# Second layer's context attention: row maxima passed through DRAM to all partitions, second scores one step later

## Chip, cores and metric

One core of a Trainium2 chip runs the kernel. The metric is the device time of one execution in microseconds.

## What is computed

Two layers of a Perceiver on 8 batches of 128 latent rows of width 512, with a context of 2048 rows a batch. The change lies in the second layer's attention from the latents to the context, 16 heads of 32:

```
q = query @ Wq.T + bq;  k = key @ Wk.T + bk;  v = value @ Wv.T + bv
scores = einsum('bhtd,bhsd->bhts', q, k) / sqrt(32)
attn = softmax(scores, axis=-1)
out = einsum('bhts,bhsd->bhtd', attn, v) @ Wo.T + bo
```

`query` is the normalised state x, `key` and `value` are the context, and the result is added to x.

## The kernel before

`softmax_context` (L1228) cuts the work into 32 units (`NU`): a batch b and a group g of four heads (`HG` = 4, r below). A unit has four chunks c of 512 context rows, so there are 128 steps n = 4u + c. All arithmetic is fp32. Each engine walks a list of tiles that `pe_step` (L1288), `act_step` (L1298) and `dve_step` (L1304) write out by step; semaphores join them.

TensorE's step: "score" (L1484), the scores of the four heads with the queries on the partitions, four matmuls of 512 columns into the four banks `score[r]`; "key" (L1540) of the next unit; in the first step of a unit "spread" (L1557) of the unit before; "score_t" (L1501), the same scores again of the unit before with the keys on the partitions, 16 products into the same four banks; "value" (L1548) of the next unit; "attend" (L1518), five steps behind its scores (`LAG`). "sums" (L1560) come in a unit's second step, "output" (L1575) in the third step of a batch's second unit, "hidden" and "query" in the third unit. A score waits for the shift that read its bank, a second score for the maximum that did.

Why twice: the softmax needs each query's maximum. "max" (L1423) takes minus the maximum of each chunk on VectorE, one number a query, so a partition. The second scores have queries along the free dimension, so the maxima must stand along it, on every partition. "diagonal" (L1427) takes the minimum over the chunks, multiplies it into the identity, and the spread multiplies ones by that diagonal: a bank with each row's number on all partitions, which ScalarE copies into `shift` (L1398). "shift" (L1435) then adds it to the second scores on VectorE, 128x512 a head, into `weights_t` (3 slots), "exp" (L1394) raises them on ScalarE in place, attend uses them, and GpSimd adds them up over the context into `partial` (L1384 to L1388), two units deep. The sums of that, by TensorE, are inverted in "heads" (L1447), which also frees `attended` for the next unit.

Keys, spreads, values, sums and the rest pass through one ring of three banks. Keys have 9 slots, values 12. In 56 of the 128 pairs of unit and chunk the values were made in earlier layers, and SyncE loads them from DRAM (`load_values`, L1334), 256 KB a pair; it also loads the next batch's context, 1 MB a chunk.

Of the kernel before, what the change touches and what calls it, by code (L numbers as in the profile page):

```python
# [16 lines left out]
P = 128  # L17
B = 8
D = 512
# [174 lines left out]
def broadcast(row):  # L194

    return row.partition_broadcast(P)
# [1031 lines left out]
def softmax_context(nc, x_sb, ident, a, ahead, own, later):  # L1228
# [7 lines left out]
    KEYS, VALUES, SLOTS = 9, 12, 3  # L1236
    with ExitStack() as ctx:
# [10 lines left out]
        diagonal = s.sb("diagonal", [P, HG, P])  # L1248
        shift = s.sb("shift", [P, 2, HG, P])
# [21 lines left out]
        diagonal_set = s.sem("diagonal_set")  # L1271
# [3 lines left out]
        value_landed = [s.sem(f"value_landed{n}") for n in range(4)]  # L1275
        chain, chain_pool = s.sem("chain"), s.sem("chain_pool")
        LOADS = 3 + 1
        LAG = NCH + 1
# [9 lines left out]
        def pe_step(n):  # L1288
            u, c = divmod(n, NCH)
            b, g = divmod(u, NG)  # L1290
            out = [("score", u, c)] * (u < NU) + [("key", u + 1, c)] * (u + 1 < NU)
            out += [("sums", u - 2)] * (c == 1 and u >= 2) + [("spread", u - 1)] * (c == 0 and 1 <= u <= NU)
            out += [("score_t", u - 1, c)] * (1 <= u <= NU) + [("value", u + 1, c)] * (u + 1 < NU)
            out += [("attend", (n - LAG) // NCH, (n - LAG) % NCH)] * (0 <= n - LAG < NU * NCH)
            out += [("hidden", b + 1)] * (g == 2 and c == 1 and b + 1 < B) + [("query", b + 1)] * (g == 2 and c == 2 and b + 1 < B)
            return out + [("output", b - 1)] * (g == 1 and c == 2 and b >= 1)

        def act_step(n):  # L1298
            u, c = divmod(n, NCH)
            exps = [("exp", u - 1, c, r) for r in range(HG)] * (1 <= u <= NU)  # L1300
            out = [("key", u + 1, c)] * (u + 1 < NU) + [("spread", u - 1)] * (c == 0 and 1 <= u <= NU)
            return out + exps[:2] + [("value", u + 1, c)] * (u + 1 < NU) + exps[2:]

        def dve_step(n):  # L1304
            u, c = divmod(n, NCH)
            b, g = divmod(u, NG)
            out = [("max", u, c, r) for r in range(HG)] * (u < NU) + [("heads", u - 2)] * (c == 1 and u >= 2)
            out += [("shift", u - 1, c, r) for r in range(HG)] * (1 <= u <= NU)
            out += [("diagonal", u)] * (c == NCH - 1 and u < NU)
            out += [("norm", b + 1)] * (g == 1 and c == 0 and b + 1 < B)  # L1310
            out += [("later", b - 1)] * (g == 1 and c == 3 and b >= 1)
            out += [("hidden", b + 1)] * (g == 2 and c == 1 and b + 1 < B) + [("query", b + 1)] * (g == 2 and c == 2 and b + 1 < B)
            return out + [("output", b - 1)] * (g == 1 and c == 2 and b >= 1)
# [9 lines left out]
                          lambda t: "a" if t[0] in ("key", "value", "spread") else "d")  # L1323

        with nc.Block() as block:

            @block.sync
            def _(sp):
# [5 lines left out]
                def load_values(k):  # L1334
# [5 lines left out]
                    if k >= 4:  # L1340
                        sp.wait_ge(value_landed[k % 4], 16 * (k // 4))
                    if n >= VALUES:
# [3 lines left out]
                                 ahead.dram[j][:, g * D:(g + 1) * D]).then_inc(value_landed[k % 4], 16)  # L1346
# [44 lines left out]
            def _(act):  # L1391
                for t in act_steps:
# [21 lines left out]
            def _(dve):  # L1414
# [5 lines left out]
                for t in dve_steps:  # L1420
# [6 lines left out]
                    elif what == "diagonal":  # L1427

                        dve.wait_ge(maxed, (u + 1) * NCH * HG)
                        link(nc.vector.tensor_reduce(row_min[:], neg_max[:, e], AX.X, ALU.min))  # L1430
                        if u:
                            dve.wait_ge(full_a, ring.count(("spread", u - 1)))
                        nc.vector.tensor_tensor(diagonal[:], ident[:].unsqueeze(1).broadcast_to([P, HG, P]),
                                                row_min[:].unsqueeze(2).broadcast_to([P, HG, P]), ALU.mult).then_inc(diagonal_set, 1)
                    elif what == "shift":  # L1435
# [3 lines left out]
                        if c == 0 and r == 0:  # L1439
                            dve.wait_ge(out_a, ring.count(("spread", u)))  # L1440
                        if n >= SLOTS and r == 0:
# [4 lines left out]
                                                shift[:, e, r, :].unsqueeze(1).broadcast_to([P, DC, P]), ALU.add).then_inc(shifted, 1)  # L1446
# [31 lines left out]
            def _(pe):  # L1478
# [3 lines left out]
                for t in pe_steps:  # L1482
                    what, u = t[0], t[1]
                    if what == "score":  # L1484
# [6 lines left out]
                        for r in range(HG):  # L1491
                            rows = slice(r * HD, (r + 1) * HD)
                            if n > NCH:

                                pe.wait_ge(shifted, (n - NCH - 1) * HG + r + 1)
                            elif n:
                                pe.wait_ge(maxed, (n - 1) * HG + r + 1)
# [3 lines left out]
                    if what == "score_t":  # L1501
# [3 lines left out]
                        for k in range(DC):  # L1505
                            for r in range(HG):
                                rows = slice(r * HD, (r + 1) * HD)
                                if k == 0 and u + 1 < NU:

                                    pe.wait_ge(maxed, (n + NCH) * HG + r + 1)  # L1510
# [7 lines left out]
                    if what == "attend":  # L1518
                        c = t[2]
                        n = u * NCH + c  # L1520
                        if (u, c) in load_no:
                            k = load_no[(u, c)]
                            pe.wait_ge(value_landed[k % 4], 16 * (k // 4 + 1))
# [644 lines left out]
```

## Time and profile before

| | |
|---|---|
| median of 3 runs | 4110.35 us (4109.7 to 4110.72) |
| the profiled execution | 4110.32 us |
| its span | 4108.5 us |
| busy over the span | TensorE 3995.8, VectorE 2177.3, ScalarE 1270.8, GpSimd 1003.8 us |
| first key to last output of this layer | about 2519 to 3819 us |

The span is what the instructions cover; 1.8 us lie around it. The busy shares are means over seven stages with different limits, so the stage itself is looked at: which engine has no idle time in it, and which waits end last. Times in the rows are from the span's start. A row of the order in time that merges several instructions runs from the first one's start to the last one's end.

### The profile page before, as it was taken

Reading aid. Unit: us, or ns where it says so; the run is one execution under the profiler, and the core shown is the slowest. Engines: PE = TensorE matmul, PEld = TensorE weight load, DVE = VectorE, ACT = ScalarE, POOL = GpSimd, SP = SyncE. Lnnn points to the kernel's source line nnn. Section 1 sums busy time; section 2 is a strip of 40 time slices with the busy share of each in tenths; the row PEclk is TensorE's granted clock in tenths of the full one; section 3 lists DMA queues with packets and bytes.
Section 4 is the critical chain, followed back from the end, with each engine's and each line's share of the span. In section 5 each row is a group of like instructions: output and inputs, shape, how many; then the busy total and the mean of one; then the engine's idle time right before and its main releaser. Section 6 shows DMA issues by size and latency. Waiting matters only on the chain. (4 is left out here: it accounts for less than half of the span.)

```text
span 4108.5 us, 73501 instructions
## 1 busy us (share of the span) xinstructions
PE 3995.8 (97%) x30656; PEld 2736.5 (67%) x30656; DVE 2177.3 (53%) x4381; ACT 1270.8 (31%) x3156; POOL 1003.8 (24%) x831
## 2 busy tenths in 40 slices
PE   8999999999999999899899999999999999998897
PEld 4777777777777778677465445666666666666675
DVE  5555555555555555255544324566665665546356
ACT  2222222222323222144233100333333333333344
POOL 2020202020202020022211000454454454445322
PEclk9999999999999999999999999999999999999899
DMA  4111111111111122211311400101101101101000
GB/s 144 62 62 62 62 62 62 62 62 62 62 61 63 58 66 73 88 29 35 108 42 48 163 0 29 55 24 45 58 24 45 58 25 45 50 1 45 11 2 21
DMA packets 127303, 219.86 MB, mean 54 GB/s; under 512 B 9088, under 2 KB 47616, under 8 KB 125184
## 3 DMA queue, kind: packets, MB, share of 16 engines
q1 hardware_dynamic: 118272, 181.60, 13.5%
q0 software_dynamic: 8704, 33.56, 2.5%
q8 instruction: 247, 4.05, 0.4%
q14 instruction: 80, 0.66, 0.1%
HBM read 198.35 MB, written 16.78 MB: 52 GB/s over the span
## 5 line engine op out<-in xcount | busy, mean ns | idle before, releaser
L577 PE MATMUL swishmax_attended<-swishmax_weights_t,swishmax_context 128*128 128x128 f32 x4096 | 520.1, 275 | 3.4 <-DVE swishmax_values_t L505 3.4
L1386 POOL TENSOR_TENSOR context_partial<-context_partial,context_weights_t 128x512 f32<-128x512 f32 x320 | 404.6, 1264 | 470.4 <-ACT context_weights_t L1397 452.7
L577 PEld LDWEIGHTS swishmax_attended<-swishmax_weights_t,swishmax_context 128*128 128x128 f32 x4096 | 487.9, 192 | 3.9 <-issue 3.9
L1546 PE MATMUL context_bank<-ahead_stream,ahead_staged 128*128 128x512 f32 x1024 | 473.3, 605 | 1.3 <-PEq L1072 1.3
L591 PE MATMUL swishmax_bank<-ahead_stream,ahead_w 128*128 128x512 f32 x1024 | 464.0, 596 | 7.2 <-DMA ahead_stream<-in_context_t_dram 7.2
L1445 DVE TENSOR_TENSOR context_weights_t<-context_score,context_shift 128x512 f32<-128x512 f32 x512 | 317.7, 683 | 231.9 <-PE context_score L1513 231.9
L435 ACT ACTIVATE swishmax_xes<-swishmax_score,swishmax_neg_max 128x512 f32<-128x512 f32 x256 | 177.2, 694 | 808.2 <-DVE swishmax_neg_max L470 808.2
L1426 DVE TENSOR_REDUCE context_neg_max<-context_score 128x1 f32<-128x512 f32 x512 | 317.9, 683 | 161.7 <-PE context_score L1498 161.4
L577 PE MATMUL swishmax_attended<-swishmax_weights_t,swishmax_sides 128*128 128x128 f32 x3072 | 384.9, 275 | 0.0
L1546 PEld LDWEIGHTS context_bank<-ahead_stream,ahead_staged 128*128 128x128 f32 x1024 | 184.0, 189 | 279.8 <-issue 272.2
L577 PEld LDWEIGHTS swishmax_attended<-swishmax_weights_t,swishmax_sides 128*128 128x128 f32 x3072 | 363.6, 192 | 0.0
L1397 ACT ACTIVATE context_weights_t<-context_weights_t 128x512 f32<-128x512 f32 x512 | 304.9, 629 | 181.8 <-DVE context_weights_t L1445 181.8
L591 PEld LDWEIGHTS swishmax_bank<-ahead_stream,ahead_w 128*128 128x128 f32 x1024 | 186.0, 192 | 198.8 <-issue 196.5
L409 POOL TENSOR_TENSOR swishmax_values_t<-swishmax_pair 128x256 f32<-128x256 f32 x32 | 23.4, 730 | 1172.3 <-ACT swishmax_pair L452 1172.2
L1405 ACT ACTIVATE context_keys_t<-context_bank,context_bias 128x512 f32<-128x512 f32 x128 | 88.0, 687 | 665.4 <-PE context_bank L1546 600.2
L1555 PE MATMUL context_bank<-ahead_w,ahead_stream 128*128 128x128 f32 x2304 | 290.4, 280 | 0.0
L1555 PEld LDWEIGHTS context_bank<-ahead_w,ahead_stream 128*128 128x128 f32 x2304 | 267.5, 192 | 18.3 <-issue 3.8
L470 DVE TENSOR_REDUCE swishmax_neg_max<-swishmax_score 128x1 f32<-128x512 f32 x256 | 164.7, 685 | 121.4 <-PE swishmax_score L562 121.4
L597 PEld LDWEIGHTS swishmax_bank<-whole_ident,swishmax_xes 128*128 128x128 f32 x1024 | 115.0, 141 | 163.7 <-issue 96.1
L475 DVE TENSOR_TENSOR swishmax_xes<-swishmax_xes,swishmax_score 128x512 f32<-128x512 f32 x256 | 175.5, 687 | 66.3 <-ACT swishmax_xes L435 66.3
L1513 PEld LDWEIGHTS context_score<-context_queries_t,context_keys_t 32*128 32x128 f32 x4096 | 132.6, 188 | 84.1 <-issue 69.9
L1387 POOL TENSOR_TENSOR context_partial<-context_partial,context_weights_t 128x512 f32<-128x512 f32 x128 | 164.3, 1284 | 10.0
(341 smaller groups left out, 5768.9 us busy)
## 6 DMA issues: line engine op xcount, KB each, us to landing
ahead_stream<-in_context_t_dram SPq DMA_DIRECT2D x78, 1024.0 KB, 5.8
swishmax_context<-in_context_dram POOLq DMA_DIRECT2D x32, 1024.0 KB, 5.9
swishmax_down<-_L_xattn_value_down_dram SPq DMA_DIRECT2D x64, 256.0 KB, 4.3
swishmax_up<-in_L_xattn_value_up_dram SPq DMA_DIRECT2D x32, 512.0 KB, 6.2
ahead_values<-ahead_staged SPq DMA_DIRECT2D x14, 1024.0 KB, 8.8
context_values<-ahead_values SPq DMA_DIRECT2D x56, 256.0 KB, 3.3
experts_w<-in_L_ffn_W_dram SPq DMA_DIRECT2D x16, 512.0 KB, 8.1
whole_x<-in_x_dram SPq DMA_DIRECT2D x8, 256.0 KB, 9.2
```

The lines of the kernel that those rows point to most:

```text
L435: nc.scalar.activation(xes[:, n % XES, r, :], score[r][:], ACT.Exp, bias=neg_max[:, e, r, c:c + 1]).then_inc(exped, 1)
L470: nc.vector.tensor_reduce(neg_max[:, e, r, c:c + 1], score[r][:], AX.X, ALU.max, negate=True).then_inc(maxed, 1)
L475: nc.vector.tensor_tensor(xe, xe, score[r][:], ALU.mult).then_inc(weighted, 1)
L577: last = nc.tensor.matmul(product(i)[:, m, :], side(left, c, k, m), weights_t[:, n % 2, right, k, :], start=c == 0 and k == 0 and m == 0 a ...
L591: last = nc.tensor.matmul(bank_t[:], w_key[:, k, g * P:(g + 1) * P], context_t[:, c, k, :], start=k == 0, stop=k == DC - 1)
L1386: link(nc.gpsimd.tensor_tensor(acc, acc, w_t[:, :, k, :], ALU.add))
L1387: nc.gpsimd.tensor_tensor(acc, acc, w_t[:, :, DC - 1, :], ALU.add).then_inc(summed, 1)
L1397: nc.scalar.activation(weights_t[:, n % SLOTS, r], weights_t[:, n % SLOTS, r], ACT.Exp).then_inc(exped, 1)
L1426: nc.vector.tensor_reduce(neg_max[:, e, r, c:c + 1], score[r][:], AX.X, ALU.max, negate=True).then_inc(maxed, 1)
L1445: nc.vector.tensor_tensor(weights_t[:, n % SLOTS, r], score[r][:].rearrange("p (k q) -> p k q", q=P), shift[:, e, r, :].unsqueeze(1).broad ...
L1546: last = nc.tensor.matmul(bank_t[:], w["k"][:, k, g * P:(g + 1) * P], context_t[:, c, k, :], start=k == 0, stop=k == DC - 1)
L1555: last = nc.tensor.matmul(bank_t[:, i * P:(i + 1) * P], context_t[:, c, k, m * P:(m + 1) * P], w["v"][:, k, g * P:(g + 1) * P], start=k == ...
```

## The change

The maxima reach the free dimension through DRAM. VectorE's "minima" step keeps the reduction into `row_min` and makes no diagonal. ScalarE's queue issues two DMAs a unit: `row_min`, 16 bytes from each of 128 partitions, to a 2 KB line in DRAM, at the start of the next unit's first step; and that line to all partitions (256 KB) into `shift`, behind that step's exponentials. The spread on TensorE and its copy on ScalarE are gone, and the ring has one tile a unit fewer. `shift` is laid out by query and then head, where it was by head and then query, so the shift reads it with a stride of four numbers. Second scores, shifts, exponentials and attend come one step later; a tenth slot of keys covers that. Sums and heads go from a unit's second to its third step, output from the third to the fourth, the gathering for the next part from the fourth to the next unit's first. The loads of values alternate between two semaphores, not four.

```diff
-    KEYS, VALUES, SLOTS = 9, 12, 3
+    KEYS, VALUES, SLOTS = 10, 12, 3
...
-        diagonal = s.sb("diagonal", [P, HG, P])
-        shift = s.sb("shift", [P, 2, HG, P])
+        minima_dram = nc.dram_tensor("context_minima", (NU, P, HG), F32, kind="Internal").ap()
+        shift = s.sb("shift", [P, 2, P, HG])
...
-        LAG = NCH + 1
+        LAG = NCH + 2
...
-            out += [("sums", u - 2)] * (c == 1 and u >= 2) + [("spread", u - 1)] * (c == 0 and 1 <= u <= NU)
-            out += [("score_t", u - 1, c)] * (1 <= u <= NU) + [("value", u + 1, c)] * (u + 1 < NU)
+            out += [("sums", u - 2)] * (c == 2 and u >= 2)
+            out += [("score_t", *divmod(n - NCH - 1, NCH))] * (0 <= n - NCH - 1 < NU * NCH) + [("value", u + 1, c)] * (u + 1 < NU)
...
+            minima = [(what, u - 1) for what in ("minima_out", "minima_in")] * (c == 0 and 1 <= u <= NU)
+            out = [("key", u + 1, c)] * (u + 1 < NU)
+            return minima[:1] + out + exps[:2] + [("value", u + 1, c)] * (u + 1 < NU) + exps[2:] + minima[1:]
...
-                    if k >= 4:
-                        sp.wait_ge(value_landed[k % 4], 16 * (k // 4))
+                    if k >= 2:
+                        sp.wait_ge(value_landed[k % 2], 16 * (k // 2))
...
-                    elif what == "spread":
-                        act.wait_ge(full_a, ring.count(t))
-                        nc.scalar.copy(shift[:, u % 2], ring.bank(t)[:].rearrange("p (r q) -> p r q", q=P)).then_inc(out_a, 1)
+                    elif what == "minima_out":
+                        act.wait_ge(minima_set, u + 1)
+                        act.dma_start(minima_dram[u], row_min[:]).then_inc(minima_landed, 16)
+                    elif what == "minima_in":
+                        act.wait_ge(minima_landed, 16 * (u + 1))
+                        act.dma_start(shift[:, u % 2].rearrange("p q r -> p (q r)"),
+                                      broadcast(minima_dram[u].rearrange("q r -> (q r)"))).then_inc(shift_landed, 16)
...
                         if c == 0 and r == 0:
-                            dve.wait_ge(out_a, ring.count(("spread", u)))
+                            dve.wait_ge(shift_landed, 16 * (u + 1))
...
-                                                shift[:, e, r, :].unsqueeze(1).broadcast_to([P, DC, P]), ALU.add).then_inc(shifted, 1)
+                                                shift[:, e, :, r].unsqueeze(1).broadcast_to([P, DC, P]), ALU.add).then_inc(shifted, 1)
...
-                    elif what == "spread":
-                        pe.wait_ge(diagonal_set, u + 1)
-                        last = nc.tensor.matmul(bank_t[:], ones[:], diagonal[:].rearrange("p r q -> p (r q)"), start=True, stop=True)
```

## Rows read from the trace of the kernel before

**Rows 1.** busy us by engine (count) in a stretch, granted clock, DMA share, GB/s.

```profile
2620.00:3740.00 1120.00, 1119.88 (x11774) 697.87 (x11776) 664.93 (x1115) 396.55 (x712) 540.61 (x426) 1.00 0.13 39
```

**Rows 2.** TensorE in order of time: start us, us, engine, line, tiles, shape, count.

```profile
2906.89 1.14 PE L1498 MATMUL context_score<-context_keys_t,context_queries_t 32*128 32x512 f32 x8
...
2915.69 1.14 PE L1498 MATMUL context_score<-context_keys_t,context_queries_t 32*128 32x512 f32 x8
...
2921.25 1.17 PE L1513 MATMUL context_score<-context_queries_t,context_keys_t 32*128 32x128 f32 x32
...
2924.34 1.08 PE L1532 MATMUL context_attended<-context_weights_t,context_values 128*32 128x128 f32 x32
...
2925.35 1.14 PE L1498 MATMUL context_score<-context_keys_t,context_queries_t 32*128 32x512 f32 x8
...
2934.50 0.66 PE L1567 MATMUL context_bank<-whole_ident,context_hidden 128*128 128x128 f32 x4
```

**Rows 3.** VectorE in order of time, the same steps; in brackets the idle time before.

```profile
2922.44 2.48 DVE L1445 TENSOR_TENSOR context_weights_t<-context_score,context_shift 128x512 f32<-128x512 f32 x4 [3.03 <-PE context_score L1513]
...
2932.06 2.48 DVE L1445 TENSOR_TENSOR context_weights_t<-context_score,context_shift 128x512 f32<-128x512 f32 x4
```

**Rows 4.** TensorE by tile: duration in ns min/median/max, first and last start us.

```profile
L1559 PE MATMUL context_bank<-context_diagonal,context_ones x64: 592/592/697, 2577.0 to 3781.8; 128*128 128x512 f32 x64
...
L1498 PE MATMUL context_score<-context_keys_t,context_queries_t x1024: 587/692/1217, 2546.4 to 3773.2; 32*128 32x512 f32 x171
```

**Rows 5.** ScalarE in order of time, the same steps.

```profile
2924.71 1.15 ACT L1397 ACTIVATE context_weights_t<-context_weights_t 128x512 f32<-128x512 f32 x2
```

**Rows 6.** VectorE by line, small instructions elsewhere, strided or not; ns as in 4.

```profile
L1154 DVE TENSOR_TENSOR experts_gap<-experts_best x2: 165/165/165, 2289.4 to 2407.1; 128x4 f32<-128x4 f32 x2
...
L1159 DVE TENSOR_TENSOR experts_prob<-experts_prob,experts_gap_exp x2: 163/164/164, 2294.3 to 2412.9; 128x4 f32<-128x4 f32 x2
...
L1788 DVE TENSOR_SCALAR features_half_norm<-features_bank x16: 183/186/193, 3839.6 to 4029.5; 128x16 f32<-128x16 f32 x16
...
L1144 DVE COPY experts_gate<-experts_bank_d x8: 166/167/168, 2285.3 to 2405.6; 128x8 f32<-128x8 f32 x8
...
L1781 DVE TENSOR_SCALAR features_inverse<-features_bank x8: 276/278/291, 3872.8 to 4062.0; 128x128 f32<-128x128 f32 x8
```

**Rows 7.** DMA issues: target, queue, count, KB, us to landing; last, value loads min/median/max.

```profile
ahead_stream<-in_context_t_dram SPq DMA_DIRECT2D x78, 1024.0 KB, 5.8
context_values<-ahead_values SPq DMA_DIRECT2D x56, 256.0 KB, 3.3
...
context_bias_o<-in_L_xattn_bo_dram SPq DMA_DIRECT2D x1, 256.0 KB, 5.0
context_bias<-in_L_xattn_bq_dram SPq DMA_DIRECT2D x1, 2.0 KB, 1.8
...
DMA to landing us min/median/max: 2.9/3.3/8.2
```

**Rows 8.** the value loads' issuing instruction on SyncE, ns min/median/max.

```profile
L1345 SPq DMA_DIRECT2D context_values<-ahead_values x56: 319/320/573, 2521.5 to 3531.2; - x56
```

**Rows 9.** the layer's end in order of time: TensorE, VectorE, GpSimd.

```profile
3752.58 2.73 PE L1513 MATMUL context_score<-context_queries_t,context_keys_t 32*128 32x128 f32 x32
...
3777.84 2.48 DVE L1445 TENSOR_TENSOR context_weights_t<-context_score,context_shift 128x512 f32<-128x512 f32 x4 [1.76 <-PE context_score L1513]
...
3783.49 2.48 DVE L1445 TENSOR_TENSOR context_weights_t<-context_score,context_shift 128x512 f32<-128x512 f32 x4 [2.36 <-PE context_score L1513]
...
3793.43 2.48 DVE L1445 TENSOR_TENSOR context_weights_t<-context_score,context_shift 128x512 f32<-128x512 f32 x4 [1.59 <-PE context_score L1513]
3796.96 2.48 DVE L1445 TENSOR_TENSOR context_weights_t<-context_score,context_shift 128x512 f32<-128x512 f32 x4 [1.04 <-PE context_score L1513]
...
3803.46 3.94 POOL L1386 TENSOR_TENSOR context_partial<-context_partial,context_weights_t 128x512 f32<-128x512 f32 x3
3807.47 1.26 POOL L1387 TENSOR_TENSOR context_partial<-context_partial,context_weights_t 128x512 f32<-128x512 f32 x1
```

More of the change, by code:

```diff
@@ L1291, in pe_step @@
             out = [("score", u, c)] * (u < NU) + [("key", u + 1, c)] * (u + 1 < NU)
[L1292 to L1293 removed]
+            out += [("sums", u - 2)] * (c == 2 and u >= 2)
+            out += [("score_t", *divmod(n - NCH - 1, NCH))] * (0 <= n - NCH - 1 < NU * NCH) + [("value", u + 1, c)] * (u + 1 < NU)
             out += [("attend", (n - LAG) // NCH, (n - LAG) % NCH)] * (0 <= n - LAG < NU * NCH)
             out += [("hidden", b + 1)] * (g == 2 and c == 1 and b + 1 < B) + [("query", b + 1)] * (g == 2 and c == 2 and b + 1 < B)
[L1296 removed]
+            return out + [("output", b - 1)] * (g == 1 and c == 3 and b >= 1)
         def act_step(n):
             u, c = divmod(n, NCH)
[L1300 to L1302 removed]
+            exps = [("exp", *divmod(n - NCH - 1, NCH), r) for r in range(HG)] * (0 <= n - NCH - 1 < NU * NCH)
+            minima = [(what, u - 1) for what in ("minima_out", "minima_in")] * (c == 0 and 1 <= u <= NU)
+            out = [("key", u + 1, c)] * (u + 1 < NU)
+            return minima[:1] + out + exps[:2] + [("value", u + 1, c)] * (u + 1 < NU) + exps[2:] + minima[1:]
         def dve_step(n):
@@ L1306, in dve_step @@
             b, g = divmod(u, NG)
-            out = [("max", u, c, r) for r in range(HG)] * (u < NU) + [("heads", u - 2)] * (c == 1 and u >= 2)
-            out += [("shift", u - 1, c, r) for r in range(HG)] * (1 <= u <= NU)
-            out += [("diagonal", u)] * (c == NCH - 1 and u < NU)
+            out = [("max", u, c, r) for r in range(HG)] * (u < NU) + [("heads", u - 2)] * (c == 2 and u >= 2)
+            out += [("shift", *divmod(n - NCH - 1, NCH), r) for r in range(HG)] * (0 <= n - NCH - 1 < NU * NCH)
+            out += [("minima", u)] * (c == NCH - 1 and u < NU)
             out += [("norm", b + 1)] * (g == 1 and c == 0 and b + 1 < B)
-            out += [("later", b - 1)] * (g == 1 and c == 3 and b >= 1)
+            out += [("later", b - 1)] * (g == 2 and c == 0 and b >= 1)
             out += [("hidden", b + 1)] * (g == 2 and c == 1 and b + 1 < B) + [("query", b + 1)] * (g == 2 and c == 2 and b + 1 < B)
-            return out + [("output", b - 1)] * (g == 1 and c == 2 and b >= 1)
+            return out + [("output", b - 1)] * (g == 1 and c == 3 and b >= 1)
         STEPS = NU * NCH + LAG + 1
@@ L1322, in softmax_context @@
                           {"a": full_a, "d": full_d}, {"a": out_a, "d": out_d},
-                          lambda t: "a" if t[0] in ("key", "value", "spread") else "d")
+                          lambda t: "a" if t[0] in ("key", "value") else "d")
         with nc.Block() as block:
@@ L1426, in _ @@
                         nc.vector.tensor_reduce(neg_max[:, e, r, c:c + 1], score[r][:], AX.X, ALU.max, negate=True).then_inc(maxed, 1)
-                    elif what == "diagonal":
+                    elif what == "minima":
                         dve.wait_ge(maxed, (u + 1) * NCH * HG)
[L1430 to L1434, printed above, removed]
+                        nc.vector.tensor_reduce(row_min[:], neg_max[:, e], AX.X, ALU.min).then_inc(minima_set, 1)
                     elif what == "shift":
@@ L1522, in _ @@
                             k = load_no[(u, c)]
[L1523 removed]
+                            pe.wait_ge(value_landed[k % 2], 16 * (k // 2 + 1))
                         else:
```

14 lines of the change are left out of this document (7 added, 7 removed).

## Prediction

> **What bounds the kernel now.** Read the busy times by stretch first, then TensorE's instructions in order of time, then VectorE's and ScalarE's over the same steps. Between 2620 and 3740 us TensorE is busy 1119.88 of 1120 us at the full granted clock, while VectorE is busy 665 and ScalarE 397 [rows 1]. So in the middle of this layer every TensorE instruction taken away shortens the run, as long as no other engine's result comes later than the place where TensorE now asks for it. The order in time [rows 2] gives the pitch of a step, score to score: 8.80 us for a plain one (2906.89 to 2915.69), 9.66 us for the one that holds the spread (2915.69 to 2925.35), and 9.15 us for the one that holds the sums (2925.35 to 2934.50). Within a plain step, counted from its score, VectorE's four shifts start 5.89 us in (2922.44 - 2915.69 - 0.86 for the spread) and take 2.48 us, so end at 8.37; with the sums they start at 6.71 (2932.06 - 2925.35) behind the reciprocal and end at 9.19 [rows 3].
>
> **Removed.** 32 spreads, two matmuls each (64 rows of the group) [rows 4]. One is worth the difference of the two pitches, 9.66 - 8.80 = 0.86 us, the rows' own gaps included [rows 2]. 30 of them (second to thirty-first unit) lie in the stretch where TensorE is never idle: 30 x 0.86 = 25.8 us. The next, in the first step of the last unit, gives nothing: the second scores behind it took 2.73 us instead of 1.17, since they waited for the maxima anyway [rows 9]. The last one is in the tail, below. The diagonal on VectorE and ScalarE's copy of the spread go too; both engines have idle time there, so I price them at nothing.
>
> **Moved.** Second scores and attend run one step later. The full stretch then lacks one group of second scores and one attend, 1.17 + 1.01 us (the group at 2921.25, and 2924.34 to 2925.35) [rows 2], which return in the tail. One more slot of keys keeps a key until its second score, 12 slots of values still suffice (an attend is then 10 steps behind its value's making, and the slot is written again 12 steps on). The heads stand in the third step instead of the second, output in the fourth, one step behind; TensorE asks for each as long after its cause as now. Value loads through two semaphores instead of four: two loads a unit of 3.3 us each against 35 us; SyncE has nothing else due then. Nothing.
>
> **Added: two DMAs a unit, on ScalarE's queue.** The first is issued at the start of a unit's first step and waits for the row minima, which VectorE makes right behind its shifts (8.4 us into the step before), when ScalarE's own exponentials are still running; no wait. Loads of the same 16 bytes a partition landed after 1.8 us [rows 7]; none was written this way, and I allow 1.8 to 3.3. The second stands behind the exponentials of that first step, 9 us later, so the first has long landed. Those exponentials end at 2924.71 + 1.15 = 2925.86, 0.5 us into the second step [rows 5]. The second DMA is a 256 KB broadcast: 3.3 us by the value loads, 5.0 us by the one broadcast row, taken while a 1 MB weight was in flight [rows 7]. A value load is released by the attend at the same moment; 1 MB takes 5.8 us, so each 256 KB more costs (5.8 - 3.3) / 3 = 0.8 us. Landing: 0.5 + 3.3 + 0.8 = 4.6 us into the second step, at most 6.3, against 5.89 when the shifts want it. Queued behind ScalarE's wait is the next key's eviction (due at 4.7), behind VectorE's the shifts and the next maxima. Issuing took SyncE 0.32 us a time [rows 8]; ScalarE has more than that free. So nothing; 0.4 us x 31 = 12 us if it always took the longest, and even that only if the slack below is used up.
>
> **Added: a strided read.** The shift is now laid out query by head, so VectorE reads 128 numbers 16 bytes apart where it read neighbours. No 512-wide row of before does that. The nearest read is a difference of two columns 32 bytes apart, 4 numbers: 165 ns, against 164 ns for the same operation on neighbours, and 163 at the least: 0.25 to 0.5 ns a number, where a doubled read would show some 1 ns for each number after the first, 3 ns. The nearest strided write, 16 numbers 16 bytes apart, took 186 ns; between the 167 ns of 8 and the 278 ns of 128 neighbours 174 would be due, so 12 ns or 0.7 ns a number more, though its two-level pattern may be part of that [rows 6]. Bounds: 0 to 1 ns a number, a shift of 683 to 1195 ns. I take the read's own row: from 0 to 0.25 ns, 683 to 811 ns.
> The Trainium skill, "SBUF — State Buffer" (section "Door 1: The DMA port swizzle", on cachelines), speaks against this: a line is 16 bytes, full bandwidth needs two hits on each, and every crossing to a new line is penalised. It also calls 4 fp32 the distance one can stride for free, which is this very stride. By the first half the slow case below comes out, by the second the forecast.
>
> **What slack the shifts have.** Four scores take 1.14 us [rows 2] and one alone 0.69 [rows 4], so the last of them starts 0.45 us in, and it is what waits for the last shift. In a plain step that shift may end at 8.80 + 0.45 = 9.25, in one with the sums at 9.15 + 0.45 = 9.60. Four shifts of length d take 4d - 0.25 (2.48 at 0.683). So a plain step stalls from d = 0.90 us, one with the sums from 0.785. At 811 ns the 29 steps with sums lose 0.10 us each, 3 us in all.
>
> **Tail.** Without maxima a round of shifts follows the last at 3.53 us (3793.43 to 3796.96) [rows 9]. In before's times: the last step with maxima shifts at 3777.84 as now, but one chunk earlier in the order; the extra round runs 3781.4 to 3783.8, its exponentials to 3784.5, the broadcast lands near 3787.8 and the last unit's first shifts start there, where they started 3783.5. GpSimd sets the end: 5.3 us for a chunk (3803.46 to 3807.47 + 1.26 = 3808.7) [rows 9]. It now has the extra chunk (3786.3 to 3791.6), then the heads, then the last unit: 3 additions to 3795.7, the second chunk from its exponentials at 3797.2, and three times 5.3 us to 3813.1: 4.4 us later.
> Sum: -25.8 - 2.2 + 4.4 = -23.6. On the profiled execution's own 4110.32 us (span 4108.5) that is 4086.7; the median of the three times, 4110.35, is the same.
>
> **Rivals.**
> A, slower: the strided read costs near a cycle a number. Its place is the slack above, it decides from d = 0.90 us. At 1195 ns four shifts take 4.53 us: stalls of 5.89 + 4.53 - 9.25 = 1.17 us in 90 plain steps and 6.71 + 4.53 - 9.60 = 1.64 in 29, so 105 + 48, and about 14 in the eight rounds of the tail: 167 on 4087 gives 4254. At the write row's 0.7 ns, d = 1.04: 0.56 and 1.03 us, 50 + 30 + 11: 4178. For it: the write row [rows 6]. Against it: the read row shows a third of it or less, but on 4 numbers, which a buffer could hide; so I hold it nearly as likely.
> B, between: d from 0.785 to 0.95 us. The 29 steps, then the rest, lose what the spreads gave: 4090 to 4115.
> C, slower: the broadcast lands late. A plain step stalls once it lands past 5.89 + 0.88 = 6.8, 6.3 us after its issue. The slowest value load took 8.2 us [rows 7]: 1.9 us x 31 = 59, 4146. Against it: 3.3 is the median and the queues are mostly empty.
> D: the spreads were hidden behind something that keeps the pitch, 4108 or so. Against it stand the pitches themselves.
>
> **How the numbers follow.** Forecast (read free or nearly) 0.50, own range 4081 to 4094 (ends: the free and the 811 ns read, the tail between nothing and 8 us). A 0.38, B 0.06 (a third of it within the measurable), C 0.04, D 0.02. The range has to take in A: 4081 to 4260. A measurement of this kernel tells 0.2% (8 us) from no change. Faster 0.54, same 0.04, slower 0.42.
>
> **What the profile after would show.** Line of the shifts: 683 to 811 ns confirms the forecast, near 1200 rival A, with TensorE's first scores waiting for it. A plain and a first step of a unit both at 8.8 us confirm the 0.86. A wait of the shifts for a DMA in a unit's second step means C. The last additions of GpSimd near 4 us later against the last unit's first scores confirm the tail. The forecast falls if the read's price was hidden by the shortness of the only row I have.

## The result, and the profile of the changed kernel

The changed kernel takes 4229.35 us (4223.37 to 4235.58, 4 runs), the kernel before beside it 4110.02 (4109.48 to 4110.72): 1.0293 times as long, interval 1.028 to 1.0306. The forecast was 4087, with 4081 to 4260 as its range. The profiled execution has a span of 4226.2 us, 117.7 more than before's 4108.5.

The page's busy times, then the middle of the layer (columns as in [rows 1]), then the waits with total us, times and longest:

```profile
PE 4115.1 (97%) x30592; PEld 2787.6 (66%) x30592; DVE 2358.0 (56%) x4349; ACT 1270.7 (30%) x3124; POOL 1005.3 (24%) x831
...
2620.00:3740.00 1120.00, 1119.85 (x10649) 668.62 (x10647) 756.16 (x989) 364.91 (x630) 500.77 (x394) 1.00 0.15 45
...
PEld context_score L1499 <- DVE context_weights_t L1446: 77.0, 121, 0.8
...
DVE context_weights_t L1446 <- issue: 20.8, 5, 5.1
...
DVE context_weights_t L1446 <- DMA context_shift<-context_minima: 2.5, 1, 2.5
```

TensorE counts as busy for the whole 1120 us as before, but with 10649 matmuls in place of 11774. The idle times hide the stall: a matmul of the first scores takes 587 or 692 ns in most cases, as before, and where four of them ran side by side they now start one after another, so their records still cover the time. The weight loads show it: those of the first scores waited 121 times for the shifts. VectorE's busy time in the window rose from 665 to 756 us. One wait of the shifts is put down to a DMA, 2.5 us; five more of 3.2 to 5.1 us, put down to "issue", are looked at below.

The shifts by tile (ns min/median/max), the two DMAs' issues, and the time to landing of the broadcast and of the DMA to DRAM:

```profile
L1446 DVE TENSOR_TENSOR context_weights_t<-context_score,context_shift x512: 1033/1087/1189, 2586.9 to 3925.2; 128x512 f32<-128x512 f32 x171
L1404 ACTq DMA_DIRECT2D context_shift<-context_minima x32: 325/326/327, 2581.1 to 3901.3; - x32
DMA to landing us min/median/max: 3.0/3.2/8.3
...
L1401 ACTq DMA_DIRECT2D context_minima<-context_row_min x32: 326/326/348, 2574.6 to 3896.3; - x32
DMA to landing us min/median/max: 1.4/1.9/4.8
```

TensorE and VectorE in order of time, which answers [rows 2] and [rows 3]: start, duration, instructions:

```profile
2904.98 2.42 PE L1499 MATMUL context_score<-context_keys_t,context_queries_t 32*128 32x512 f32 x8
2907.33 3.70 PE L1547 MATMUL context_bank<-ahead_stream,ahead_staged 128*128 128x512 f32 x8
...
2915.05 2.40 PE L1499 MATMUL context_score<-context_keys_t,context_queries_t 32*128 32x512 f32 x8
...
2925.11 2.43 PE L1499 MATMUL context_score<-context_keys_t,context_queries_t 32*128 32x512 f32 x8
...
2902.07 4.15 DVE L1446 TENSOR_TENSOR context_weights_t<-context_score,context_shift 128x512 f32<-128x512 f32 x4 [3.53 <-PE context_score L1514]
...
2906.33 0.33 ACTq L1401 DMA_DIRECT2D context_minima<-context_row_min  x1
...
2916.32 0.33 ACTq L1404 DMA_DIRECT2D context_shift<-context_minima  x1
```

The spread is gone and the first step of a unit (2904.98 to 2915.05) is as long as the plain one after it, but both take 10.07 us where a plain step took 8.80. The four first scores last 2.42 us instead of 1.14: each writes the bank that a shift still reads, and waits for that shift. A shift takes 1087 ns (median) where it took 681. That is rival A.

Rival C, the late broadcast, has a small part in it. Each of the five waits put down to "issue" ends 0.08 us after a broadcast has landed. One of them, from the DMA's issue to TensorE's first scores:

```profile
2959.74 0.33 ACTq L1404 DMA_DIRECT2D context_shift<-context_minima  x1
...
2968.08 4.04 DVE L1446 TENSOR_TENSOR context_weights_t<-context_score,context_shift 128x512 f32<-128x512 f32 x4 [5.05 <-issue]
...
2969.33 4.79 PE L1499 MATMUL context_score<-context_keys_t,context_queries_t 32*128 32x512 f32 x8
```

Four broadcasts in the middle of the layer landed after 7.1 to 8.3 us instead of 3.2. The first scores behind them last 3.06 to 4.79 us, where the same steps of the kernel before with the strided read (below) have 2.27 to 2.29: 5 us in all. The other two waits lie in the last unit.

### The profile page after: what moved, and what is told of

Read it like the earlier page. It is cut to its first block and busy times, and to the rows that moved or that the text cites. A ratio compares the mean times of both kernels' runs of the same rounds, so it can differ in the third digit from the quotient of the medians.

```text
span 4226.2 us, 73312 instructions
## 1 busy us (share of the span) xinstructions
PE 4115.1 (97%) x30592; PEld 2787.6 (66%) x30592; DVE 2358.0 (56%) x4349; ACT 1270.7 (30%) x3124; POOL 1005.3 (24%) x831
## 5 line engine op out<-in xcount | busy, mean ns | idle before, releaser
L1446 DVE TENSOR_TENSOR context_weights_t<-context_score,context_shift 128x512 f32<-128x512 f32 x512 | 527.5, 1097 | 288.6 <-PE context_score L1514 265.2
L1387 POOL TENSOR_TENSOR context_partial<-context_partial,context_weights_t 128x512 f32<-128x512 f32 x320 | 407.1, 1272 | 560.4 <-ACT context_weights_t L1398 542.7
L1398 ACT ACTIVATE context_weights_t<-context_weights_t 128x512 f32<-128x512 f32 x512 | 321.3, 631 | 350.3 <-DVE context_weights_t L1446 346.2
L1499 PE MATMUL context_score<-context_keys_t,context_queries_t 32*128 32x512 f32 x1024 | 281.4, 652 | 1.0 <-DVE context_queries_t L1469 0.9
L1514 PEld LDWEIGHTS context_score<-context_queries_t,context_keys_t 32*128 32x128 f32 x4096 | 142.4, 195 | 88.1 <-issue 69.7
```

The lines of the kernel that those rows point to most:

```text
L1387: link(nc.gpsimd.tensor_tensor(acc, acc, w_t[:, :, k, :], ALU.add))
L1398: nc.scalar.activation(weights_t[:, n % SLOTS, r], weights_t[:, n % SLOTS, r], ACT.Exp).then_inc(exped, 1)
L1446: nc.vector.tensor_tensor(weights_t[:, n % SLOTS, r], score[r][:].rearrange("p (k q) -> p k q", q=P), shift[:, e, :, r].unsqueeze(1).broad ...
L1499: nc.tensor.matmul(score[r][:], queries_t[rows, b % 2, g, :], keys_t[rows, n % KEYS, :], start=True, stop=True).then_inc(scored, 1)
```

## Experiments

**Neighbours again.** The changed kernel, with `shift` laid out by head and then query. The transposition is left to the DMA to DRAM, which then writes single numbers.

```diff
-        minima_dram = nc.dram_tensor("context_minima", (NU, P, HG), F32, kind="Internal").ap()
-        shift = s.sb("shift", [P, 2, P, HG])
+        minima_dram = nc.dram_tensor("context_minima", (NU, HG, P), F32, kind="Internal").ap()
+        shift = s.sb("shift", [P, 2, HG, P])
...
-                        act.dma_start(minima_dram[u], row_min[:]).then_inc(minima_landed, 16)
+                        act.dma_start(minima_dram[u].rearrange("r q -> q r"), row_min[:], allow_slow_non_contiguous=True).then_inc(minima_landed, 16)
```

> The changed kernel with the shift laid out head by query again: the first DMA writes 4-byte pieces to turn the layout on its way to DRAM, the second and all else stay. Theory S (the strided read is the whole loss): a shift is back at 683 ns, the pitch of a plain step at 8.80 us from 10.07, and the time at 4087 us (4081 to 4094). Rival M (the move by one step, the DMAs or ScalarE's issuing of them cost): shifts at 683 ns but the time stays above 4110, up to the 4229 of the changed kernel.

4099.34 us (4094.06 to 4103.87), ratio 0.9974 [0.9965, 0.9984]: 130 us are back, and the shift takes 680 ns. It is still some 12 us above the forecast. The DMA of 512 single numbers lands late, and ScalarE's queue stands still for it; the first unit and the last:

```profile
2574.91 0.40 ACTq L1401 DMA_DIRECT2D context_minima<-context_row_min  x1
...
2583.26 0.34 ACTq L1404 DMA_DIRECT2D context_shift<-context_minima  x1
...
2588.33 1.89 DVE L1446 TENSOR_TENSOR context_weights_t<-context_score,context_shift 128x512 f32<-128x512 f32 x3 [3.40 <-DMA context_shift<-context_minima]
...
3774.86 0.33 ACTq L1404 DMA_DIRECT2D context_shift<-context_minima  x1
...
3778.11 2.48 DVE L1446 TENSOR_TENSOR context_weights_t<-context_score,context_shift 128x512 f32<-128x512 f32 x4 [10.02 <-issue]
```

In the first unit the second DMA is issued 8.35 us after the first, when that has landed (in the changed kernel it lands after 1.9 us at the median), and the shifts wait 3.40 us for the broadcast; in the last unit it is issued 10.2 us after the first, and they wait 10.02. Against the pairs kernel (below) 6.6 us are lost before the last unit and 6.0 in it. So this layout gives back on the DMA a part of what it saves on VectorE; it shows the read's price, but not the change at its best.

**The stride in the kernel before.** Only the layout of `diagonal` and `shift` is changed, to query by head; spreads and order stay.

```diff
-        diagonal = s.sb("diagonal", [P, HG, P])
-        shift = s.sb("shift", [P, 2, HG, P])
+        diagonal = s.sb("diagonal", [P, P, HG])
+        shift = s.sb("shift", [P, 2, P, HG])
...
-                                                shift[:, e, r, :].unsqueeze(1).broadcast_to([P, DC, P]), ALU.add).then_inc(shifted, 1)
+                                                shift[:, e, :, r].unsqueeze(1).broadcast_to([P, DC, P]), ALU.add).then_inc(shifted, 1)
```

> The kernel before with only the layouts of the diagonal and of the shift turned to query by head, so that the shift reads with a stride of 16 bytes; the spread, its copy and the order of steps stay. Theory S: a shift takes about 1.09 us, as in the changed kernel; a plain step goes from 8.80 to 10.07 us, and the time to 4229 + 23 = 4252 us (4235 to 4265). Rival M: within 10 us of 4110, whatever the shift's length, since TensorE has 0.88 us of slack in a plain step by the prediction's working.

4246.92 us, ratio 1.033 [1.0314, 1.0345], without any DMA of the change. The shift takes 1091 ns. So the strided read alone costs 137 us in the old order; between the changed kernel and the pairs (below) lie 146, the late broadcasts' 5 us among them.

**Pairs.** The changed kernel with `shift` as two pairs of heads, `[P, 2, 2, P, 2]`: a shift reads every second number, 8 bytes apart, and the DMA writes 8 bytes at a time.

```diff
-        shift = s.sb("shift", [P, 2, P, HG])
+        shift = s.sb("shift", [P, 2, 2, P, 2])
...
-                        act.dma_start(minima_dram[u], row_min[:]).then_inc(minima_landed, 16)
+                        act.dma_start(minima_dram[u].rearrange("h q r -> q h r"), row_min[:].rearrange("p (h r) -> p h r", r=2)).then_inc(minima_landed, 16)
...
-                                                shift[:, e, :, r].unsqueeze(1).broadcast_to([P, DC, P]), ALU.add).then_inc(shifted, 1)
+                                                shift[:, e, r // 2, :, r % 2].unsqueeze(1).broadcast_to([P, DC, P]), ALU.add).then_inc(shifted, 1)
```

> The changed kernel with two heads interleaved instead of four, so that the shift reads with a stride of 8 bytes. If what costs is the crossing from one 16-byte line to another on every number: two numbers a line, a shift near 683 ns and the time near 4087 us. If any stride costs: a shift near 1.09 us and 4229. If the cost grows with the number of lines touched: half way, about 0.89 us a shift, and some 4120.

4083.4 us (4082.04 to 4084.73), ratio 0.9935 [0.992, 0.995]; run again later, 4082.35 (4081.76 to 4085.08), ratio 0.9931 [0.9917, 0.9946]:

> The kernel with two heads interleaved, a second time and beside the one with the shorter tail: 4083 us again, 0.6 to 0.7% under the kernel before.

The shifts, then two steps of TensorE in order of time:

```profile
L1446 DVE TENSOR_TENSOR context_weights_t<-context_score,context_shift x512: 673/680/693, 2584.0 to 3775.7; 128x512 f32<-128x512 f32 x171
...
2904.89 1.14 PE L1499 MATMUL context_score<-context_keys_t,context_queries_t 32*128 32x512 f32 x8
...
2913.69 1.14 PE L1499 MATMUL context_score<-context_keys_t,context_queries_t 32*128 32x512 f32 x8
```

A read 8 bytes apart is free (673 to 693 ns). The first step of a unit is at 8.80 us, as forecast, with both DMAs in place. This is the forecast's own case, and 4 us from its number.

**Only one step later.** The kernel before, its spreads and its copy kept, with the changed kernel's order and ten slots of keys.

```diff
-    KEYS, VALUES, SLOTS = 9, 12, 3
+    KEYS, VALUES, SLOTS = 10, 12, 3
...
-        LAG = NCH + 1
+        LAG = NCH + 2
...
-            out += [("score_t", u - 1, c)] * (1 <= u <= NU) + [("value", u + 1, c)] * (u + 1 < NU)
+            out += [("score_t", *divmod(n - NCH - 1, NCH))] * (0 <= n - NCH - 1 < NU * NCH) + [("value", u + 1, c)] * (u + 1 < NU)
```

> The kernel before with the second scores, shifts, exponentials, attend, sums, heads and output one step later and a tenth slot of keys, and nothing else: spread and diagonal stay. Theory S: 4110 us plus or minus 5 (2.2 us less in the full stretch, one more round of about 3.5 us in the tail, and GpSimd's last chunks behind it). Rival M: 4125 or more, with new waits of TensorE for VectorE in the third step of a unit.

4108.06 us, ratio 0.9997 [0.9988, 1.0007]: nothing. Counted from the layer's first key, the last unit starts 3.2 us earlier than before, and from there its last sums come 5.5 us later. The gain of the pairs is the spreads', not the order's.

**VectorE time without a stride.** The kernel before, with an unused sum of 256 neighbouring numbers ahead of each shift (its result goes nowhere).

```diff
+                        link(nc.vector.tensor_tensor(unused[:], score[r][:, 0:2 * P].rearrange("p (k q) -> p k q", q=P),
+                                                     ones[:].unsqueeze(1).broadcast_to([P, 2, P]), ALU.add))
```

> The kernel before, with 256 numbers added by VectorE into an unused tile ahead of each shift, all reads on neighbours: about 0.42 us more a head, where the strided read costs 0.41. Theory S says that only VectorE's time between the second scores and the next first scores counts: about the time of the kernel before with the strided read, 4245 to 4265 us, with a plain step near 10.1 us. Rival R (the strided read also slows what runs beside it, GpSimd, ScalarE or TensorE): clearly less than that kernel.

The added sum took 414 ns, what the stride adds; the kernel 4276.71 us, ratio 1.0402 [1.0385, 1.042]. So it needs no contention to lose the time: 0.41 us more for VectorE before each score's bank is free does it. It lost 29 us more than the stride did. A round of four sums and shifts takes 4.3 us where four strided shifts take 4.1, and 16 of the 29 lie in the first scores (137 us longer than in the pairs kernel, 121 with the stride). Another 10 lie in the keys, and why is not shown.

**The price by stride.** The kernel before, with instructions of 512 numbers at its end, three of each kind, whose results go nowhere; the edit shown is the one that reads 16 bytes apart. Sums of a bank and a strided operand, by line: the operand's numbers 4, 12, 16 and 32 bytes apart; then the same sum written 4 and 16 bytes apart; last ScalarE's copy reading 4, 8, 12 and 16 bytes apart.

```diff
+                for _ in range(3): link(nc.vector.tensor_tensor(narrow[:, 0:512 * 1].rearrange("p (q s) -> p q s", s=1)[:, :, 0], bank_a[0][:], wide[:, 0:512 * 4].rearrange("p (q s) -> p q s", s=4)[:, :, 0], ALU.add))
```

> The kernel before, with single VectorE and ScalarE instructions of 512 numbers added at the very end of its last part, three of each, on one engine at a time: a sum of a PSUM bank and an SBUF row read at strides of 1, 2, 3, 4, 5, 6 and 8 numbers, the same written at strides of 1, 2, 4 and 8, a maximum and a copy read at 1, 2, 4 and 8, and ScalarE's copy read and written so. If lines of 16 bytes are what costs: 1 and 2 near 683 ns, 3 between, 4 and more near 1.09 us and all alike; by the row of the four numbers 32 bytes apart all would be under 0.81. A write at 4 near 1.0 us by the row of the sixteen. The time of the whole is the kernel before plus the added instructions.

```profile
L2040 DVE TENSOR_TENSOR nets_hidden<-nets_bank_a,nets_units x3: 683/691/692, 4103.9 to 4105.4; 128x512 f32<-128x512 f32 x3
L2042 DVE TENSOR_TENSOR nets_hidden<-nets_bank_a,nets_units x3: 826/827/830, 4108.3 to 4110.0; 128x512 f32<-128x512 f32 x3
L2043 DVE TENSOR_TENSOR nets_hidden<-nets_bank_a,nets_units x3: 1049/1049/1049, 4110.9 to 4113.0; 128x512 f32<-128x512 f32 x3
L2046 DVE TENSOR_TENSOR nets_hidden<-nets_bank_a,nets_units x3: 1065/1066/1066, 4120.6 to 4122.8; 128x512 f32<-128x512 f32 x3
...
L2048 DVE TENSOR_TENSOR nets_hidden<-nets_bank_a,nets_units x3: 691/691/692, 4127.2 to 4128.6; 128x512 f32<-128x512 f32 x3
L2050 DVE TENSOR_TENSOR nets_hidden<-nets_bank_a,nets_units x3: 1058/1058/1059, 4131.5 to 4133.7; 128x512 f32<-128x512 f32 x3
...
L1985 ACT COPY nets_hidden<-nets_units x3: 617/617/617, 4155.8 to 4157.1; 128x512 f32<-128x512 f32 x3
L1986 ACT COPY nets_hidden<-nets_units x3: 648/648/649, 4157.7 to 4159.1; 128x512 f32<-128x512 f32 x3
L1987 ACT COPY nets_hidden<-nets_units x3: 870/871/872, 4159.8 to 4161.6; 128x512 f32<-128x512 f32 x3
L1988 ACT COPY nets_hidden<-nets_units x3: 1088/1089/1089, 4162.5 to 4164.7; 128x512 f32<-128x512 f32 x3
```

At 8 bytes the sum took 691 ns too. So: nothing to 8 bytes, 0.27 ns a number at 12, 0.70 from 16 on ((1049 - 691) / 512), and little more beyond. With the shift's own pattern, 128 strided numbers read four times over, it took 1049 ns as well. The Trainium skill, "SBUF — State Buffer" (section "Door 1: The DMA port swizzle"), has 16-byte lines that want two hits each, and these rows fit that rule: 8 bytes apart gives two to a line. They contradict the same passage's sentence that one can stride 4 fp32 for free.

**Short reads.** The same at the end of the kernel before, both inputs in SBUF and the stride 4 bytes or 32, for 4 to 256 numbers.

```diff
+                for _ in range(3): link(nc.vector.tensor_tensor(narrow[:, 0:4], wide[:, 0:32].rearrange("p (q s) -> p q s", s=8)[:, :, 0], wide[:, 0:32].rearrange("p (q s) -> p q s", s=8)[:, :, 0], ALU.add))
```

> The kernel before with short VectorE instructions added at the very end, three of each: sums with both inputs in SBUF on 4, 8, 16, 32, 64, 128 and 256 numbers at strides of 1 and 8 numbers, sums with one input in PSUM and the other read at strides of 1 and 4, and a scaling of 16 numbers written at strides of 1 and 4. If the price is the same for each number however short the row: 4 numbers 3 ns more at a stride of 8, 16 numbers 12, 256 numbers 190. If the start of an instruction hides the first of them: nothing on 4 and 8, and a price that begins at some length, which is what the row of four in the kernel before could not show. The 16 written at a stride of 4: 12 ns more if the prediction read that row rightly.

By line: 4 numbers at stride 4 bytes and 32, then 128 and 256 numbers; last, with one input in a PSUM bank as the shift has it, 16 and 256 numbers at stride 4 bytes and 16.

```profile
L2027 DVE TENSOR_TENSOR nets_hidden<-nets_units x3: 155/161/161, 4104.5 to 4104.9; 128x4 f32<-128x4 f32 x3
L2028 DVE TENSOR_TENSOR nets_hidden<-nets_units x3: 165/165/165, 4105.1 to 4105.5; 128x4 f32<-128x4 f32 x3
...
L2037 DVE TENSOR_TENSOR nets_hidden<-nets_units x3: 292/293/293, 4111.3 to 4111.9; 128x128 f32<-128x128 f32 x3
L2038 DVE TENSOR_TENSOR nets_hidden<-nets_units x3: 385/386/386, 4112.3 to 4113.1; 128x128 f32<-128x128 f32 x3
L2039 DVE TENSOR_TENSOR nets_hidden<-nets_units x3: 424/425/426, 4113.5 to 4114.5; 128x256 f32<-128x256 f32 x3
L2040 DVE TENSOR_TENSOR nets_hidden<-nets_units x3: 615/616/617, 4114.9 to 4116.2; 128x256 f32<-128x256 f32 x3
L2041 DVE TENSOR_TENSOR nets_hidden<-nets_bank_a,nets_units x3: 174/174/174, 4116.9 to 4117.3; 128x16 f32<-128x16 f32 x3
L2042 DVE TENSOR_TENSOR nets_hidden<-nets_bank_a,nets_units x3: 177/178/178, 4117.5 to 4117.9; 128x16 f32<-128x16 f32 x3
...
L2047 DVE TENSOR_TENSOR nets_hidden<-nets_bank_a,nets_units x3: 424/424/424, 4122.0 to 4122.9; 128x256 f32<-128x256 f32 x3
L2048 DVE TENSOR_TENSOR nets_hidden<-nets_bank_a,nets_units x3: 598/599/599, 4123.4 to 4124.6; 128x256 f32<-128x256 f32 x3
```

With both inputs strided, 4 numbers cost 4 ns more (medians), 128 cost 93, 256 cost 191: the price of a number, 0.7 to 1 ns, is there in full on 4 numbers. But 4 ns is little beside the 161 that the instruction takes, and the three equal runs on neighbours alone differ by 6. With one input in a bank, 16 numbers cost 4 ns more, or 0.25 each, and 256 cost 175, or 0.68: in this form the first numbers hide most of their price. Sixteen numbers written 16 bytes apart took 185 ns against 175, so the prediction read its write row rightly.

**The slack.** The kernel before with one unused sum of 512 numbers, ahead of the last shift of each step alone.

```diff
+                        if r == HG - 1:
+                            link(nc.vector.tensor_tensor(unused[:], score[r][:].rearrange("p (k q) -> p k q", q=P),
+                                                         ones[:].unsqueeze(1).broadcast_to([P, DC, P]), ALU.add))
```

> The kernel before with one sum of 512 numbers on VectorE into an unused tile ahead of the last of the four shifts of every step: about 0.75 us a step, all reads on neighbours. By the slack of the prediction (0.88 us in a plain step, 0.41 in one with the sums) only the steps with sums lose, 0.34 us x 25, so 4119 us. By a slack that ends where the next step begins (0.43 us in a plain step, nothing in one with the sums), with none in the steps made longer by output, query or the last batch's values: 0.35 us in about 62 plain steps and 0.75 in about 20, so 37 us and some in the tail, 4147 to 4155.

4151.15 us, ratio 1.0104 [1.0087, 1.0121]. TensorE's first scores behind a step without the sums and behind one with them; last, VectorE's round of four shifts in the first of these steps, with the added sum between the two rows:

```profile
2896.16 1.48 PE L1502 MATMUL context_score<-context_keys_t,context_queries_t 32*128 32x512 f32 x8
...
2905.65 1.94 PE L1502 MATMUL context_score<-context_keys_t,context_queries_t 32*128 32x512 f32 x8
...
2893.26 1.89 DVE L1449 TENSOR_TENSOR context_weights_t<-context_score,context_shift 128x512 f32<-128x512 f32 x3 [3.44 <-PE context_score L1517]
...
2895.78 0.69 DVE L1449 TENSOR_TENSOR context_weights_t<-context_score,context_shift 128x512 f32<-128x512 f32 x1
```

The added sum takes 0.68 us and makes the round 3.21 us long instead of 2.48, 0.73 more. That costs 0.34 us in a plain step and 0.80 in one with the sums. So the slack is 0.39 and none, not the 0.88 and 0.41 that the prediction used. By those, this kernel would have lost some 8 us; it lost 42 against the runs of before beside it.

**The tail.** The pairs kernel, with the last chunk of the last unit added up by VectorE into the unused half of `partial` instead of by GpSimd; the last sums take both halves.

```diff
-                for n in range(NU * NCH):
+                for n in range(NU * NCH - 1):
...
+                        if n == NU * NCH - 1 and r == HG - 1:
+                            dve.wait_ge(exped, NU * NCH * HG)
+                            w_t, acc = weights_t[:, n % SLOTS], partial[:, (u + 1) % 2]
+                            link(nc.vector.tensor_tensor(acc, w_t[:, :, 0, :], w_t[:, :, 1, :], ALU.add))
+                            link(nc.vector.tensor_tensor(acc, acc, w_t[:, :, 2, :], ALU.add))
+                            nc.vector.tensor_tensor(acc, acc, w_t[:, :, 3, :], ALU.add).then_inc(maxed, 1)
...
```

> The kernel with two heads interleaved, and its last chunk added up over the context by VectorE instead of GpSimd, into the other half of the partial sums; the last sums then take both halves. If GpSimd's backlog sets the end of the layer, as the prediction's tail has it: the last sums about 5 us sooner, 4078 us. If something else ends last there (the last attend, the exponentials), or VectorE and GpSimd slow each other on the same memory: 0 to 2 us.

4078.98 us (4077.32 to 4082.19), ratio 0.9925 [0.991, 0.9939], the fastest of all. TensorE's last sums in the pairs kernel and in this one, and VectorE's first addition:

```profile
3786.37 0.66 PE L1561 MATMUL context_bank<-context_partial,context_ones 128*32 128x128 f32 x8 [8.11 <-POOL context_partial L1388]
```

```profile
3780.30 0.68 PE L1570 MATMUL context_bank<-context_partial,context_ones 128*32 128x128 f32 x8 [3.97 <-DVE context_partial L1453]
...
3775.13 1.68 DVE L1451 TENSOR_TENSOR context_partial<-context_weights_t 128x512 f32<-128x512 f32 x1 [0.70 <-ACT context_weights_t L1398]
```

TensorE's idle time there falls from 8.11 us, waiting for GpSimd, to 3.97, waiting for VectorE. The sums come 6.1 us earlier, 1.4 of it from before this unit; some 4 us reach the end. VectorE's additions took 1.63 to 1.68 us where a shift takes 0.68; both their inputs lie in SBUF and GpSimd was adding meanwhile. The Trainium skill, "SBUF — State Buffer" (section "Who interferes with whom"), says that such a sum contends with GpSimd's reads. The kernel before agrees, in the sum of x and a bias, which also has both inputs in SBUF:

```profile
L1473 DVE TENSOR_TENSOR whole_x<-whole_x,context_bias_o x8: 692/1416/1624, 2753.2 to 3817.8; 128x512 f32<-128x512 f32 x8
```

Seven of the eight ran while GpSimd was adding and took 1.41 to 1.62 us; the last, with GpSimd at rest, took 0.69. It isn't always VectorE that loses: in the slack kernel six of the eight took 0.69 us beside GpSimd too, and there GpSimd's three additions took longer, 4.45 us instead of 3.94 (at 2916.36 us).

## Why the prediction went wrong

The forecast failed on the strided read; rival A with its place and mechanism is what happened. The account goes by the start of the last unit's first scores: 3750.45 us in before, 3720.92 in the pairs kernel and 3859.88 in the changed one. Counted from the layer's first key (2519.38, 2518.62 and 2521.51) these are 1231.1, 1202.3 and 1338.4 us. Laid out by line over this stretch, TensorE's time in the changed kernel is 136 us longer than in the pairs kernel: 124 in the first scores, 7 in the keys, 5 elsewhere.

- **Spreads, 25.8 us, and the moved work, 2.2.** Right: the last unit starts 28.8 us earlier with the pairs, where 28.0 were forecast, and the first step of a unit is 8.80 us. The kernel that only runs later has 3.2 of these, the spreads the other 25.6.
- **The two DMAs, nothing.** Right for the pairs kernel, where no shift before the last unit waited for a broadcast, in either of its two profiles. In the changed kernel the typical times are as forecast: to DRAM 1.9 us (allowed 1.8 to 3.3), the broadcast 3.2 (3.3), its issue 0.33. But the forecast let the broadcast land at most 6.3 us into the step, and four took 7.1 to 8.3 us from their issue; this is rival C in four units of 32, and cost 5 us of the 119 lost.
- **The strided read.** This step failed. I took 0 to 0.25 ns a number from a row of 4 numbers, against 0.7 from a write of 16. The short reads show why. On 4 numbers the whole price is 4 ns, and the two rows of [rows 6] differ by 1 to 2: the strided one took the probe's 165 ns, the one on neighbours 164 where the probe has 161. It was another instruction, a multiplication of other tiles, and a few ns between two instructions can't tell 0.25 ns a number from 0.7. The figure in this kernel is 0.79 ns (1087 - 681, by 512), between the write row's 0.7 and the upper bound of 1.
- **The slack.** Mis-sized too. I let the last score start 0.45 us into its group, by 1.14 us for four and 0.69 for one. But a score is two matmuls, and the four run side by side: in the pairs kernel's group at 2904.89 the first matmuls of all four heads start within 0.02 us. In the changed kernel the last shift ended at 2906.22 (2902.07 + 4.15) and the next key began at 2907.33, 1.11 us later: as long as a whole group of four that waits for nothing takes (1.07 to the key in the pairs kernel). So the group gets no head start. From key to key a plain step takes 4.82 us to the first shift, the four shifts and 1.11: with 2.48 us that is 8.41, or 0.39 under 8.80; with 4.12 it is 10.05, the measured pitch. With the sums the shifts begin at 5.64 (2933.11 - 2927.47): 9.23 with the short ones, no slack, and 10.87 with the long. Even the forecast's own upper end, 811 ns, would have cost some 0.1 and 0.6 us in these steps, not 3 us in all.
- **The count of steps.** Rival A counted 90 plain and 29 sums steps at 1195 ns. Of the 124 groups of first scores before the last unit, 65 are 1.2 to 1.3 us too long, 18 are 1.7, 7 are others (0.7 to 3.6, four of them behind late broadcasts), and 34 are not late at all: in steps that output, query, hidden or the values of the last batch make longer, TensorE comes later than the shifts. In sum 126 us. Two such steps of the last batch in the changed kernel, 10.58 us apart:

```profile
3710.10 1.14 PE L1499 MATMUL context_score<-context_keys_t,context_queries_t 32*128 32x512 f32 x8
...
3720.68 1.14 PE L1499 MATMUL context_score<-context_keys_t,context_queries_t 32*128 32x512 f32 x8
```

  So the rival's 153 us at 1195 ns and its 80 at 1040 miss in two ways that oppose each other: fewer steps stall, and each stalls longer.
- **The tail, +4.4 us.** From the last unit's start to the last sums before took 58.4 us, the pairs 65.5: +7.0, so this term was 2.6 us too small. GpSimd sets it, as said, and the pairs kernel waits 8.11 us for it. The forecast let the last round beside the maxima stand where it stood; in the pairs kernel it comes 1.7 us later in the unit (29.1 us in, against 27.4), and the extra round 4.3 us behind it, not 3.53. The changed kernel took 72.7, with each round of four shifts 1.6 us longer.
- **Behind the layer** before took 299.6 us from the last sums to the end, the pairs 293.8: 5.8 us that no term of the forecast had. It is not the later order's: the slack kernel, in the order of before, has 294.1. The granted clock differs. In the 30 us after the next part's first score it is 0.83 in before (3840 to 3870 us) and in its strided version (3978 to 4008, 298.9 us to the end), 1.00 in the slack kernel (3884 to 3914) and in the pairs (3817 to 3847). What sets the clock there no run tells, so this stays open.

For the pairs' span the sum is -0.8 ahead of the layer, -28.8, +7.0 and -5.8, which gives the measured -28.3 but for rounding. The forecast's -23.6 stands for the layer alone, where -21.8 were measured; the rest of the gain is none of its terms.

## What to carry to other kernels

Price a changed access pattern on an instruction of the size that it is used at: two rows of 4 numbers from different instructions can't rule out a price of 0.7 ns a number. Measure the slack of a waiting engine from the release to the next instruction behind the wait, step kind by step kind, since the idle column shows nothing where matmuls that used to run side by side start one by one. Where a wait is put down to "issue", look whether a DMA landed just before its end. When a DMA lays data out anew, choose a layout whose reader stays within 8 bytes (fp32 pairs), rather than one that makes the DMA simplest or the reader contiguous: here 4083 us, against 4229 and 4099.

## What was unexpected of the hardware

- VectorE reads every second fp32 at full rate (691 ns for 512), every third at 827, every fourth and on at 1049 to 1066; written the same way (691, 1058). ScalarE's copy goes 617, 648, 871, 1089 ns.
- In the layer, beside the other engines, the sum with the stride of 16 bytes took 1087 ns (at most 1189), at the kernel's end 1049; on neighbours it took 681 and 691. The repeated pattern is not the cause (1049 ns at the end too); what the 38 ns are is open.
- A 2 KB DMA to DRAM landed after 1.9 us (median) in 128 pieces of 16 bytes and after 3.4 in 256 pieces of 8; in 512 pieces of 4 the DMA that waits for it was issued 8.35 us behind it in the first unit and 10.2 in the last.
- The granted clock behind the layer came in two forms, 0.83 or 1.00 over the same 30 us of work, in kernels that differ only before it; that is about 5 us.
- VectorE's sums of 128x512 with both operands in SBUF took 0.69 us with GpSimd at rest and 1.41 to 1.68 beside a busy GpSimd, except in the slack kernel, where six took 0.69 and GpSimd's own additions grew longer.
